# An attention kernel: folds of the output weights with the upper rows ahead of the lower rows

## What is computed

```python
Q = (img_embed @ Wq).reshape(B, -1, H, D).transpose(0, 2, 1, 3)
K = (sent_embed @ Wk).reshape(B, -1, H, D).transpose(0, 2, 1, 3)
V = (sent_embed @ Wv).reshape(B, -1, H, D).transpose(0, 2, 1, 3)
score = jnp.einsum('bhqd,bhkd->bhqk', Q, K) / math.sqrt(D)
attn = jax.nn.softmax(jnp.where(mask, score, -jnp.inf), axis=-1)
ctx = jnp.einsum('bhqk,bhkd->bqhd', attn, V).reshape(B, -1, H * D)
out = ctx @ Wo + img_embed
return (out - mu) * jax.lax.rsqrt(var + EPS) * gamma + beta
```

## Time and profile before

| | us |
|---|---|
| median of 3 runs | 312.84 |
| lowest and highest | 312.39 and 313.38 |
| the profiled execution's own time | 312.59 |
| its span, first to last instruction | 310.8 |

### The profile page before, as it was taken

How to read it: one execution, slowest core, us unless ns; L and a number is a source line. 1 busy time by engine, 2 the same in 40 slices (tenths; PEclk the granted TensorE clock), 3 DMA queues, 4 the chain that set the end, 5 groups by cost and what they waited for, 6 DMA issues and landing times.

```text
span 310.8 us, 8035 instructions
## 1 busy us (share of the span) xinstructions
PE 304.6 (98%) x2570; PEld 298.0 (96%) x2570; DVE 243.9 (78%) x696; ACT 228.2 (73%) x615; POOL 201.2 (65%) x209
## 2 busy tenths in 40 slices
PE   8999999999999999999999999999999999999994
PEld 6898888999999999999999999999999999999994
DVE  0457778778998779787989879877988889877676
ACT  2546678768888687878887887868797797868760
POOL 1123476556868588857868487858878487857811
PEclk9999999999999999999999999999999999999999
DMA  7996444473354644574346543474455444543301
GB/s 248 367 404 257 138 137 153 144 218 114 95 167 144 208 154 135 175 249 139 114 147 190 185 148 118 164 232 135 135 172 181 155 141 147 166 149 124 84 2 68
DMA packets 48143, 51.32 MB, mean 165 GB/s; under 512 B 3584, under 2 KB 38144, under 8 KB 48128
## 3 DMA queue, kind: packets, MB, share of 16 engines
q1 hardware_dynamic: 47840, 50.61, 49.2%
q10 hardware_dynamic: 288, 0.52, 0.6%
HBM read 32.77 MB, written 18.35 MB: 164 GB/s over the span
## 4 chain that ended last, share of the span: by engine, by line
PE 96%; DMA 2%; DVE 1%; SPq 0%; POOLq 0%; issue 0%; POOL 0%
PE score_bank L346 25%; PE out_bank L346 19%; PE gL_bank L346 14%; PE tL_bank L346 13%; PE tU_bank L346 9%; PE gU_bank L346 7%; DMA wq_raw<-in_wqT 2%; PE spare_bank L346 1%; PE spare_bank L380 1%; PE tL_bank L380 1%; PE tL_bank L362 1%; PE tU_bank L362 1%; PE out_bank L386 1%; PE tU_bank L386 1%; PE spare_bank L362 0%; PE out_bank L362 0%
## 5 line engine op out<-in xcount | busy, mean ns | idle before, releaser
L1055 POOL TENSOR_TENSOR probs<-probs,inv_sum 128x512 f32<-128x512 f32 x64 | 66.7, 1043 | 63.1 <-DVE inv_sum L859 62.8
L651 ACT ACTIVATE probs<-neg_scores,neg_max 128x256 f32<-128x256 f32 x128 | 64.1, 502 | 32.3 <-DVE neg_max L848 32.3
L1098 POOL TENSOR_TENSOR pT_lo<-pT_raw,pT_hi 128x512 fp32r<-128x512 f32 x62 | 79.3, 1302 | 10.0 <-ACT pT_hi L607 10.0
L848 DVE CUSTOM_DVE_ANT_0 neg_scores<-score_bank,mask_bias 128x256 f32<-128x256 f32 x128 | 49.2, 422 | 6.7 <-PE score_bank L346 4.2
L869 DVE STREAM_TRANSPOSE squares<-probs 128x512 f32<-128x512 f32 x62 | 43.8, 706 | 0.3
L794 DVE TENSOR_TENSOR tL_lo<-tL_bank,tL_hi 128x512 fp32r<-128x512 f32 x30 | 20.8, 692 | 23.9 <-ACT tL_hi L607 23.9
L607 ACT ACTIVATE tL_hi<-tL_bank 128x512 fp32r<-128x512 f32 x30 | 17.9, 598 | 24.7 <-PE tL_bank L346 24.5
L607 ACT ACTIVATE pT_hi<-pT_raw 128x512 fp32r<-128x512 f32 x62 | 35.4, 623 | 0.0
L346 PE MATMUL gL_bank<-xT_hi,A_lo 128*128 128x256 f32 x128 | 35.3, 276 | 0.0
L346 PE MATMUL gL_bank<-xT_hi,A_hi 128*128 128x256 f32 x128 | 35.3, 276 | 0.0
L346 PE MATMUL gL_bank<-xT_lo,A_hi 128*128 128x256 f32 x128 | 35.3, 276 | 0.0
(11 more groups left out here) (192 smaller groups left out, 1010.7 us busy)
## 6 DMA issues: line engine op xcount, KB each, us to landing
scratch<-squares SPq DMA_DIRECT2D x31, 512.0 KB, 2.6
pT_raw<-scratch SPq DMA_DIRECT2D x124, 128.0 KB, 3.1
xT_raw<-in_xT SPq DMA_DIRECT2D x8, 256.0 KB, 3.2
ctxT_raw<-in_ctxT SPq DMA_DIRECT2D x8, 256.0 KB, 3.5
wo_raw<-in_wo SPq DMA_DIRECT2D x4, 512.0 KB, 14.8
x_res<-in_x SPq DMA_DIRECT2D x8, 256.0 KB, 3.0
out<-y SPq DMA_DIRECT2D x7, 256.0 KB, 2.7
wq_raw<-in_wqT SPq DMA_DIRECT2D x3, 512.0 KB, 7.6
```

The costliest lines, as they stand in the source:

```text
L651: nc.scalar.activation(probs[j % 2][:, n, :], neg_scores[:, n, :], ACT.Exp, bias=neg_max[:, n:n + 1], scale=-1.0, accum_out=row_sum[:, n:n ...
L848: nc.vector.tensor_tensor_reduce(out=neg_scores[:, n, :], in0=score_bank[hh][:, q, :], in1=mask_bias[:], scale=-SCALE, scalar=3.0e38, op0= ...
L1055: nc.gpsimd.tensor_tensor(probs[j % 2][:, rows, :], probs[j % 2][:, rows, :], inv, ALU.mult) \
L1098: nc.gpsimd.tensor_tensor(pT_lo[j % 2][:, k].rearrange("p hh (q i r) -> p (hh q) i r", q=QT, i=ROWS), pT_raw[j % 2][:, k].rearrange("p i n ...
```

## The change

In `fold_C` the four matmuls of the upper rows come first and the four of the lower rows second, and with them the meaning of the two steps of C_product. ACT's and DVE's splits are turned to match: CU first, CL second. The number of instructions, their operands and banks and every count that others wait for are the same.

```diff
@@ fold_C (TensorE)
                 for hh in range(2):
                     h = 2 * j + hh
                     for d in range(DT):
-                        ins = nc.tensor.matmul(lower[:, hh, :], wv_raw[:, h * DT + d, 0:P],
+                        ins = nc.tensor.matmul(upper[hh * UP:(hh + 1) * UP, 0, :],
+                                               wv_raw[:, h * DT + d, P:DL],
                                                wo_raw[:, h * DT + d, :], start=d == 0, stop=d == DT - 1)
                 ins.then_inc(C_product, 1)
                 for hh in range(2):
                     h = 2 * j + hh
                     for d in range(DT):
-                        ins = nc.tensor.matmul(upper[hh * UP:(hh + 1) * UP, 0, :],
-                                               wv_raw[:, h * DT + d, P:DL],
+                        ins = nc.tensor.matmul(lower[:, hh, :], wv_raw[:, h * DT + d, 0:P],
                                                wo_raw[:, h * DT + d, :], start=d == 0, stop=d == DT - 1)
                 ins.then_inc(C_product, 1)
@@ C_hi_part (ACT)
                 act.wait_ge(C_product, 2 * j + 1)
+                hi_part(CU_hi[:, j, :], upper[:, 0, :]).then_inc(C_hi_done, 1)
+                act.wait_ge(C_product, 2 * j + 2)
                 hi_part(CL_hi[:, 2 * j:2 * j + 2, :], lower[:]).then_inc(C_hi_done, 1)
-                act.wait_ge(C_product, 2 * j + 2)
-                hi_part(CU_hi[:, j, :], upper[:, 0, :]).then_inc(C_hi_done, 1)
@@ C_lo_part (DVE)
                 dve.wait_ge(C_hi_done, 2 * j + 1)
+                lo_part(CU_lo[:, j, :], upper[:, 0, :], CU_hi[:, j, :]).then_inc(C_split, 1)
+                dve.wait_ge(C_hi_done, 2 * j + 2)
                 lo_part(CL_lo[:, 2 * j:2 * j + 2, :], lower[:], CL_hi[:, 2 * j:2 * j + 2, :]).then_inc(C_split, 1)
-                dve.wait_ge(C_hi_done, 2 * j + 2)
-                lo_part(CU_lo[:, j, :], upper[:, 0, :], CU_hi[:, j, :]).then_inc(C_split, 1)
```

## The result

The changed kernel took 322.36 us (321.94 to 322.76, 4 runs) beside 312.67 for the kernel before on the same chips: 1.0302 times as long, with a 95% interval from 1.0284 to 1.0319. It is 9.7 us slower, far outside the range. The profiled execution took 322.33 us, its span is 320.5.

The account below looks back on a forecast made before the run. TensorE, busy 98% of the span, was taken as the bound; four folds at 3.06 us against 3.06 summed to 0.0 us, so 312.8 us was forecast, range 312.2 to 313.9.

Parts of the forecast that it names:

- The fold itself: TensorE's four folds of C after the first four steps' query products: 3.06 us each before and after, 0.0 us in all.
- The values taken between the bounds: Fold's new transitions: 0.20 into uppers, 0.31 plus 0.11 into lowers, 0.22 out; all bounds together allowed -0.8 to +1.2 us.
- ACT, DVE and the banks: Turned splits fit existing idle time, fold 0's maximum stays at 28.00, and nobody waits for CL or CU singly.
- The slack of 0.24 us ahead of step 3's scores: DVE's gU split ends at 40.57, scores start at 40.81; TensorE would wait only if splits ended over 0.24 us later.
- the prediction's own signs: Forecast wrong if fold stretches differ by over 0.2 us each, or TensorE's later steps show a new wait.
- the rest of the kernel can only be shifted by what those pieces do: Only the four folds after the first four steps' query products, 12.2 us in all, can be reordered.
- The unseen pair: Last lower (4-byte) to next step's first rounded instruction, both 128 wide: plain 0.22, extra cost 0, bounds 0 and 0.20.
- Rival 1: In the folds, the two heads' uppers no longer start together: 0.44 us a fold, 1.8 in all, 314.6; chance 0.05.
- Rival 2: In the folds, pairs not seen before cost their upper bounds: +1.2 us, 314.1; chance of both 0.05.
- rival 3: In the folds, unseen pairs at their bottom: -0.8 us, 312.0; chance of a gain over 0.3% 0.03.

Follow-up runs that it names:

- e2: Against the changed kernel: TensorE folds lowers first as before; ACT and DVE wait for both products and split CU first; 312.74 us.
- e6: Changed kernel with one small 64-column matmul of zeros between steps 5 and 6; 322.49 us.
- e8: Kernel before with one wide 4-byte matmul of zeros over 128 columns behind the old fold 3; 322.91 us.
- e3: Kernel before with folds 0 to 2 in the new order, splits included, and fold 3 in the old; 312.72 us.
- e11: Changed kernel with EARLY (number of steps whose scores read g_early) set from 5 to 6; 313.00 us.
- e12: Kernel before with EARLY set from 5 to 4, so step 4's scores read gL and gU, folds untouched; 322.63 us.
- e13: Kernel before with g_early exchanged with gL_hi, gL_lo and gU in the order of allocation; 316.66 us.
- e14: Changed kernel with g_early exchanged with gL_hi, gL_lo and gU in the order of allocation; 316.21 us.
- e7: Kernel before with one small 64-column matmul of zeros between steps 5 and 6; 321.87 us.
- e9: Kernel before with one small 64-column matmul of zeros between steps 4 and 5; 322.06 us.
- e1: Against the changed kernel: TensorE still folds uppers first; ACT and DVE wait for both products and split CL first, as before; 322.35 us.
- e4: Kernel before with only fold 3 in the new order, splits included; 322.57 us.

## Why the prediction was wrong

- **The fold itself: right.** Three of the four stretches are 3.06 us, with 0.21 (forecast 0.20) into the uppers, 0.38 ahead of the lowers and, with the score's exposed load, 0.22 out of them. The values taken between the bounds were the right ones. Fold 2's stretch of 3.50 holds the wait for the late store.
- **ACT, DVE and the banks: right for the splits**, and e2 shows their order to be worth nothing. The slack of 0.24 us ahead of step 3's scores was used up by a slow store, which the prediction hadn't in its sum: 0.44 us. By the prediction's own signs this wait counted against it, but e2 and e6 show that it comes and goes without regard to the folds' order.
- **The step that failed** is the first paragraph's: "the rest of the kernel can only be shifted by what those pieces do". It takes a rounded matmul's spacing for a constant. It is one of two constants, 0.1133 and 0.1178, and the way out of fold 3 chose between them for 2128 matmuls: 2128 x 0.00444 = 9.45 us, out of a place where the sum for the fold was right to a hundredth. No bound on the fold's own cost could have held it, since all were bounds on a piece of 12.2 us.
- **The unseen pair.** "Last lower to the next step's first instruction" was named as the pair that never occurs freely in the trace, and was bounded by what it costs there (0 to 0.20). Its own cost is 0. What it does to the stream behind it is the whole result, and e8 shows that this pair alone is enough there. In folds 0 to 2 the same pair is harmless (e3).
- **The rivals.** Rival 1 (column groups apart) is refuted: the uppers took 1.09. Rival 2 (unseen pairs at their upper bounds) is refuted as well, and rival 3 (at their lower bounds) too, by the 3.06. The slower side was held for possible, at 0.10, but with mechanisms inside the fold.
- **The trace of before had the sign.** Its scores ran at 0.120 and its query products at 0.113 with the same shapes, and the first query products at 0.118 with the same stationary tiles as those made in step 3 for step 4. One kind of matmul with three spacings is a question to be answered before a sum is made with one of them.

## What to carry to other kernels

Where TensorE is the bound and runs thousands of equal matmuls, compare the spacing from start to start in a steady stretch before and after any edit to its stream, even one far away: a loss that is spread evenly over instructions that the edit doesn't touch, with no idle time and the clock unchanged, is a changed rhythm and not a cost of the edit. Such an edit is judged by where it leaves the stream and not only by its own length. If the slow rhythm is met, change what runs last ahead of the steady part (here: one more step of scores from the upper tile, e11), and look at the spacing again, since the same scores in e11's step 4 did not help.

## What the runs showed of the hardware

- A stream of rounded 4-byte matmuls (a load of 128 columns and 256 streamed columns each) has two steady spacings, 0.1133 and 0.1178 us, at the same granted clock of 1.00. Either one held over 2128 matmuls, through loop branches and semaphore waits that don't stall. The Trainium skill (TensorE: Matmul & The Clock Gate, Back-to-back issue gap) gives N/2.4 + 2.5 ns for the gap of an isolated matmul, by which an estimate for 256 columns is 109 ns. It says that in a stream of loads and matmuls both set the spacing. Both spacings of this stream lie above the 109 ns; no run here shows the isolated gap.
- Scores whose stationary tile lies at 95 KB of a partition, with ctxT at 105 KB, run at 0.120, evenly or, where they don't settle, on average; with the tile at 83 KB at 0.113 or 0.118 (e12, e13, e14). The first 12 output products behind the transposes, which read other tiles, settle at 0.120 too, in both kernels. Which part of the address decides was not tried.
- A switch from 128 to 64 columns and back (in e7 0.206 us from the last rounded start to the small matmul, and 0.258 more to the next rounded start) broke the fast rhythm in e7 and e9. A wide 4-byte matmul followed without a gap by a rounded one, behind fold 3, was followed by the slow one in the changed kernel, e1, e4, e6, e8 and (until step 5) e11; in e14, whose step 4 reads its scores' tile from the lower place, it was followed by the fast one.
- Why the unit that loads and the one that streams settle in the one or the other rhythm isn't shown by these runs. That it is the phase of the loads against the matmuls is a conjecture: between 100 and 250 us a load starts 3 or 4 ns after the start of the matmul ahead of it in the fast rhythm (the old kernel), and 2 or 3 ns in the slow one (the changed kernel).
